# Turning the FFNs' attention probabilities with transposing transfers instead of TensorE transposes

## The chip, the cores and the metric

One core of one Trainium2 chip runs the whole kernel. The metric is device microseconds of one execution, the median of three runs. TensorE is called PE, VectorE DVE, ScalarE ACT, GpSimd POOL, SyncE SP; a "tile" is a block of 128 tokens.

## The reference, cut to what matters

```python
x = x + 0.5 * ffn(layernorm(x))
x = x + attn(layernorm(x))
x = x + 0.5 * ffn(layernorm(x))          # x: (8, 512, 256), float32

def ffn(h):                              # 16 experts, hidden size C = 256, H = 128
    w = gates(h)                         # (tokens, 16): softmax over the active experts
    def mix(proj):                       # proj: (16, C, H)
        pe = einsum('nc,ech->neh', h, proj)
        return einsum('ne,neh->nh', w, pe)
    q, k, v = mix(q_proj), mix(k_proj), mix(v_proj)
    scores = where(causal, einsum('bqh,bkh->bqk', q, k) / sqrt(H), -1e9)
    ao = einsum('bqk,bkh->bqh', softmax(scores), v)
    return einsum('enh,ehc->nc', einsum('ne,nh->enh', w, ao), o_proj)
```

Each of the two FFNs is itself an attention of one head whose projections are mixtures of 16 experts. The 16-head attention between them is not touched.

## The kernel before

Three programs follow each other: `ffn` (FFN 1), `attention`, `ffn` again (FFN 2). x stays in SBUF throughout. Products that need float32 accuracy are made of fp32r high and low halves, three matmuls each.

**An FFN as a pipeline of slots.** There are 32 tiles (8 batch items of QT = 4 tiles) and 34 slots. Slot T works on several tiles at once, and the order on each engine is written out by hand in that engine's `slot(T, t)`: a loop over e = 0 to 15, the experts, into which the steps of other tiles are set at fixed e. In slot T, PE does

- `mix(T, t, e)` (L555) for e = 1 to 15: six matmuls of 384 columns for tile T, into a ring of four PSUM banks that DVE empties with `sum_mix` (L725, L727);
- at every odd e, `project(T - 2, ..., e // 2, ...)` (L605): three matmuls of 512 columns, the output projection of tile T - 2, which DVE adds up in `sum_output` (L742, L744, L746). The first of them, at e = 1, waits for `av_lo`, the low half of that tile's attention output;
- at e = 0 `transpose_y` and at e = 2 `mix_first` for tile T + 1;
- the small causal attention of tile T - 1: `transpose_qk` at e = 4, `scores` at e = 6, `transpose_probs` (L583) at e = 9, `attend` (L593) at e = 12. "t" of a tile is its number within its batch item, 0 to 3; its scores have (t + 1) * 128 columns.

**The chain of tile T - 1 within slot T.** PE scores (e = 6); DVE `score_max` (L759, e = 7); ACT `exponentials` (L902), into `prob`, float32 in SBUF; PE `transpose_probs` turns `prob` into PSUM, t + 1 blocks of 128 by 128; ACT `split_probs` (L908, high half) and DVE `split_probs` (L765, e = 10, low half) bring them to `probT` in SBUF; PE `attend` (e = 12); DVE `sum_av` (L779, L783, e = 13) adds the two halves of the result; POOL `split_av` (L1026, L1028) makes the halves `avT`; and in slot T + 1, at e = 1, PE's first `project` reads `avT`. A tile's probabilities are unnormalised; 1 / sum goes into the output weights `w_out`.

POOL's order in a slot: `merge_qkv` and `split_v` of tile T - 1, the gate's steps for tile T + 1, `split_av(T - 1)`, `merge_x(T - 2)` (L1033). SP first loads all weights, in FFN 1 then the first pieces of the attention's weights when their space is free, and in FFN 2 stores each batch item when its four tiles are merged.

**In `attention`** the probabilities are turned already by transposing transfers: ACT (L1556) and DVE (L1479) write `probs` as two fp16 halves scaled by 2^15, SP issues `dma_start_transpose` (L1294) into `turned_long` (14 blocks of 128 columns, 1792) and `turned_short` (6 blocks, 768), and POOL casts them to fp32r (L1614).

Of the kernel before, what the change touches and what calls it, by code (L numbers as in the profile page):

```python
# [47 lines left out]
ON_POOL = (5, 7, 13)  # L48

# [220 lines left out]

def lo_of(n):

    if n in ON_POOL:
        return "pool", ON_POOL.index(n) + 1
    return "dve", n + 1 - sum(i < n for i in ON_POOL)


def ffn(nc, m, name, aw, sim_matrix, gates, q_proj, k_proj, v_proj, o_proj, x_in, out):
    with ExitStack() as ctx:
# [25 lines left out]

        stats = sb("ln_stats", [P, 2, 6])
# [37 lines left out]
        prob = sb("prob", [P, SEQ])  # L344
        p_sum = sb("prob_sum", [P, 1])
        p_rsum = sb("prob_rsum", [P, 1])
        pT = sb("probT", [P, QT, 2, P], F32R)
# [30 lines left out]
        pt_tr, pt_hi, pt_lo, av_ready = sem("pt_tr"), sem("pt_hi"), sem("pt_lo"), sem("av_rdy")  # L378
# [54 lines left out]
        def _(sp):  # L433
# [43 lines left out]
            if aw:  # L477
                for n in range(EARLY):
                    if n == 0:
                        split_done(sp, E + OG - 2)  # L480
                        split_done(sp, E + OG - 1)
                    if n == 2:
                        last_tile_past(sp, aw.first_end)
                    if n == EARLY - 2:
                        last_tile_past(sp, aw.second_end)
                    src, _, _, _, width = aw.pieces[n]
                    raw = aw.parts(n)[0]
                    sp.dma_start(raw, src).then_inc(aw.loaded[n % EARLY], 16)
            if out is not None:
                out_rows = out.rearrange("b (t p) c -> b p t c", p=P)  # L490
                with sp.Fori(0, B) as b:
                    sp.wait_ge(x_merged, b * QT + QT)
                    sp.dma_start(out_rows[bass.ds(b, 1)].rearrange("a p t c -> p (a t) c"),
                                 m.x[:, bass.ds(b * QT, QT), :]).then_inc(stored, 16)
                sp.wait_ge(stored, 16 * B)

        @block.tensor
        def _(pe):
# [136 lines left out]
        def _(dve):  # L635
# [156 lines left out]
            def slot(T, t):  # L792
                nxt, prev, nn = (t + 1) % QT, (t + 3) % QT, (t + 2) % QT
                for e in range(E):
# [33 lines left out]
                    if inside(T, 1):  # L828
                        if e == 4:
                            split_qk(T - 1, prev)  # L830
                        if e == 7:
                            score_max(T - 1, prev)
                        if e == 9:
                            prob_rsum(T - 1, prev)
                        if e == 10:
# [3 lines left out]
                        if e == 13:  # L839
# [34 lines left out]
        def _(act):  # L874
# [44 lines left out]
            def slot(T, t):  # L919
                for e in range(E):  # L920
# [12 lines left out]
                    if e == 9 and inside(T, 1):  # L933
# [22 lines left out]
        def _(pool):  # L956
# [65 lines left out]

            def split_av(T, t):
# [16 lines left out]
            def slot(T, t):  # L1040
# [21 lines left out]
                if inside(T, 1):  # L1062
                    split_av(T - 1, prev)
# [25 lines left out]
PROB_SCALE = 2.0 ** 15  # L1089
# [597 lines left out]
```

## Time and profile before

| | |
|---|---|
| median of 3 runs | 2614.89 us (2613.47 to 2616.02) |
| profiled execution | 2615.02 us |
| its span in the trace | 2613.2 us |
| TensorE busy | 2511.2 us (96%) |
| VectorE busy | 2155.9 us (83%) |
| ScalarE, GpSimd busy | 945.1 us (36%), 910.6 us (35%) |
| transposing transfers, from issue to landing | 4.0 us (1792 columns), 3.5 us (768 columns), medians |

A profile comes from one execution. Busy time is the share of the span in which an engine runs an instruction. PE's matmuls are pipelined: what one costs is the distance between the starts of groups that follow each other, not its own duration. "[x <- engine tile line]" behind a row is the idle time before it and what ended it.

### The profile page before, as it was taken

The numbers are of one execution on the slowest core, as the hardware profiler recorded it, in microseconds if no ns is written. First come the engines' busy times: TensorE is split into PE (matmuls) and PEld (weight loads), VectorE is DVE, ScalarE is ACT, GpSimd is POOL, SyncE is SP. The second block draws the span as 40 slices with busy tenths as digits, with TensorE's granted clock in tenths as the row PEclk, the third lists the DMA queues.
The fourth block names the chain that finished last, engine by engine and source line by source line (L and its number), as shares of the span: only waits on it lengthen the run. The fifth ranks groups of instructions, "written<-read, shape, count | busy, mean of one in ns | idle before, by whom it ended". The sixth has DMA issues, their size and how long they took to land. (4 is left out here: it accounts for less than half of the span.)

```text
span 2613.2 us, 45221 instructions
## 1 busy us (share of the span) xinstructions
PE 2511.2 (96%) x14116; PEld 2298.0 (88%) x14116; DVE 2155.9 (83%) x6164; ACT 945.1 (36%) x2546; POOL 910.6 (35%) x1950
## 2 busy tenths in 40 slices
PE   6999999999996899999999999997999999999998
PEld 6999999999995788888888888886899999999997
DVE  6888888888886888888888888886888888888887
ACT  3111101101102777777777777774111101101100
POOL 4332332332323444343434344334332332332321
PEclk9999999999998999999999999997999999999999
DMA  6000000000001554454545554455100000000000
GB/s 191 11 1 1 1 1 1 1 1 1 1 25 49 91 92 91 86 94 90 87 92 91 92 92 91 85 98 127 34 9 1 9 9 1 9 9 1 9 9 9
DMA packets 378735, 117.25 MB, mean 45 GB/s; under 512 B 338560, under 2 KB 377472, under 8 KB 378496
## 3 DMA queue, kind: packets, MB, share of 16 engines
q1 hardware_dynamic: 378496, 114.36, 21.9%
q8 instruction: 114, 1.87, 0.3%
q14 instruction: 125, 1.02, 0.1%
HBM read 26.24 MB, written 4.19 MB: 12 GB/s over the span
## 5 line engine op out<-in xcount | busy, mean ns | idle before, releaser
L555 PE MATMUL ffn_ring<-ffn_mix_weights,ffn_yT 128*128 128x384 f32 x5760 | 1155.7, 341 | 6.7 <-DVE ffn_mix_weights L790 4.3
L555 PEld LDWEIGHTS ffn_ring<-ffn_mix_weights,ffn_yT 128*128 128x128 f32 x5760 | 1007.4, 189 | 57.5 <-DVE ffn_mix_sums L725 15.8
L727 DVE SCALAR_TENSOR_TENSOR ffn_mix_sums<-ffn_ring,ffn_w,ffn_mix_sums 128x384 f32<-128x384 f32 x896 | 550.3, 614 | 243.0 <-PE ffn_ring L555 226.1
L605 PE MATMUL ffn_ring<-ffn_out_weights,ffn_avT 128*128 128x512 f32 x1536 | 442.3, 399 | 6.2 <-POOL ffn_avT L1028 4.5
L1547 ACT ACTIVATE attn_exponentials<-attn_exponentials,attn_score_neg_max 128x512 f32<-128x512 f32 (+3 forms) x512 | 285.8, 559 | 173.5 <-DVE attn_score_neg_max L1462 172.9
L1614 POOL CAST attn_probsT_long<-attn_turned_long 128x1024 fp32r<-128x1024 f16 (+1 forms) x256 | 232.4, 936 | 248.0 <-DVE attn_probs L1479 246.8
L605 PEld LDWEIGHTS ffn_ring<-ffn_out_weights,ffn_avT 128*128 128x128 f32 x1536 | 282.8, 189 | 36.0 <-POOL ffn_avT L1028 5.7
L1479 DVE SCALAR_TENSOR_TENSOR attn_probs<-attn_exponentials,attn_prob_factor,attn_probs 128x512 f16<-128x512 f32 (+3 forms) x512 | 254.0, 557 | 20.2 <-ACT attn_probs L1556 19.9
L1556 ACT ACTIVATE attn_probs<-attn_exponentials,attn_prob_factor 128x512 f16<-128x512 f32 (+3 forms) x512 | 250.2, 552 | 23.1 <-DVE attn_prob_factor L1472 13.8
L742 DVE SCALAR_TENSOR_TENSOR x<-ffn_ring,ffn_w_out,x 128x256 f32<-128x256 f32 x512 | 246.9, 482 | 12.0 <-PE ffn_ring L605 5.3
L1302 PE MATMUL attn_scores<-attn_kT,attn_qT 128*128 128x512 f32 (+2 forms) x1152 | 243.2, 338 | 9.1 <-DVE attn_qT L1445 7.6
L1462 DVE CUSTOM_DVE_ANT_0 attn_exponentials<-attn_scores,causal_row 128x512 f32<-128x512 f32 (+2 forms) x384 | 205.5, 551 | 32.1 <-PE attn_scores L1341 24.0
L1302 PEld LDWEIGHTS attn_scores<-attn_kT,attn_qT 128*128 128x128 f32 x1152 | 197.8, 189 | 38.2 <-DVE attn_qT L1445 8.0
L1302 PE MATMUL attn_dense<-attn_wd,attn_ctxT 128*128 128x256 f32 x1512 | 202.0, 283 | 20.6 <-DVE attn_ctxT L1486 19.4
L1302 PEld LDWEIGHTS attn_dense<-attn_wd,attn_ctxT 128*128 128x128 f32 x1512 | 185.4, 189 | 31.4 <-DVE attn_ctxT L1486 29.3
L746 DVE SCALAR_TENSOR_TENSOR ffn_out_odd<-ffn_ring,ffn_w_out,ffn_out_odd 128x256 f32<-128x256 f32 x448 | 212.7, 475 | 0.0
L1614 POOL CAST attn_probsT_short<-attn_turned_short 128x512 fp32r<-128x512 f16 (+1 forms) x256 | 122.9, 508 | 232.7 <-DVE attn_probs L1479 232.7
L1302 PE MATMUL attn_projections<-attn_zT,early_wq 128*128 128x512 f32 x768 | 201.8, 398 | 1.5 <-DVE attn_zT L1447 1.5
L884 ACT ACTIVATE ffn_yT<-ffn_transposes 128x256 fp32r<-128x256 f32 x64 | 24.5, 383 | 493.2 <-PE ffn_transposes L525 493.2
L888 ACT ACTIVATE ffn_qT<-ffn_transposes 128x128 fp32r<-128x128 f32 x64 | 17.7, 277 | 441.4 <-PE ffn_transposes L565 441.4
L1302 PE MATMUL attn_ctx<-attn_probsT_long,attn_v 128*128 128x512 f32 (+1 forms) x768 | 167.3, 366 | 0.0
L1026 POOL CAST ffn_avT<-ffn_av 128x128 fp32r<-128x128 f32 x64 | 19.5, 304 | 420.7 <-DVE ffn_av L783 420.7
(149 smaller groups left out, 3263.1 us busy)
## 6 DMA issues: line engine op xcount, KB each, us to landing
ffn_mix_stage<-in_L_ffn_q_proj_dram SPq DMA_DIRECT2D x32, 128.0 KB, 2.5
ffn_mix_stage<-in_L_ffn_k_proj_dram SPq DMA_DIRECT2D x32, 128.0 KB, 2.6
ffn_mix_stage<-in_L_ffn_v_proj_dram SPq DMA_DIRECT2D x32, 128.0 KB, 2.9
ffn_out_stage<-in_L_ffn_o_proj_dram SPq DMA_DIRECT2D x16, 256.0 KB, 3.2
out_dram<-x SPq DMA_DIRECT2D x8, 512.0 KB, 2.9
x<-in_L_attn_x_dram SPq DMA_DIRECT2D x7, 512.0 KB, 8.2
early_stage<-in_L_attn_w_q_dram SPq DMA_DIRECT2D x4, 512.0 KB, 5.7
attn_dense_stage<-in_L_attn_w_dense_dram SPq DMA_DIRECT2D x4, 512.0 KB, 4.7
```

What stands on the lines that cost most here:

```text
L555: last = pe.matmul(bank[:, 0:QKV], yT[:, t % 2, h, k * P:(k + 1) * P], mix_half(e, wh)[:, k], start=(n == 0), stop=(n == 3 * CK - 1))
L605: last = pe.matmul(bank[:], avT[:, t % 2, h], wo[:, g, wh], start=(i == 0), stop=(i == 2))
L727: dve.scalar_tensor_tensor(into, bank[:, 0:QKV], w[:, t, e:e + 1], into, ALU.mult, ALU.add).then_inc(mix_done, 1)
L742: dve.scalar_tensor_tensor(x, bank[:, 0:C], wt[:, 2 * g:2 * g + 1], x, ALU.mult, ALU.add)
L746: dve.scalar_tensor_tensor(odd[:, t % 2], bank[:, C:2 * C], wt[:, 2 * g + 1:2 * g + 2], odd[:, t % 2], ALU.mult, ALU.add).then_inc(out_don ...
L884: act.activation(yT[:, t % 2, 0], tr[:, 0:C], ACT.Copy).then_inc(yT_hi, 1)
L1302: mm = pe.matmul(out_ap, stationary(a), moving(c), start=first and n == 0, stop=last and n == 2, skip_group_check=True)
L1462: dve.tensor_tensor_reduce(expo[:, at:at + width], raw, row, -1.0, BIGGEST, ALU.add, ALU.min, s_bias[:, h % 2, i:i + 1]).then_inc(s_max, 1)
L1479: dve.scalar_tensor_tensor(prob_half(1, i), expo[:, at:at + width].rearrange("p (j k) -> p j k", k=P), p_factor[:, h % 2, i:i + 1], prob_h ...
L1547: act.activation(expo[:, at:at + width], expo[:, at:at + width], ACT.Exp, bias=s_bias[:, h % 2, i:i + 1], scale=-1.0, accum_out=p_sum[:, h ...
L1556: act.activation(prob_half(0, i), expo[:, at:at + width].rearrange("p (j k) -> p j k", k=P), ACT.Copy, scale=p_factor[:, h % 2, i:i + 1]). ...
L1614: pool.tensor_copy(cast(n, i), landed(n, i).rearrange("p (j h q) -> p j h q", h=HL, q=P)).then_inc(long_cast if pair_of(i) else short_cast, 1)
```

## The change

In each FFN, tiles 1 to 30 (`by_dma(T)`) take another path; tiles 0 and 31 keep the old one.

- PE: `transpose_probs` is left out for them, and `attend` moves from e = 12 to e = 14.
- ACT: `split_probs` is replaced by `prob16_high` at e = 8: `prob` times 2^15 as fp16, from SBUF to SBUF. It waits for the exponentials.
- DVE: `split_probs` at e = 10 is replaced by `prob16_low` at e = 9, the fp16 remainder; `sum_av` moves from e = 13 to e = 15. `w_out` takes the factor 2^-15.
- SP: `turn_probs(T)`, one `dma_start_transpose` of 2 (t + 1) blocks of 128 columns, after `pt_lo`.
- POOL: `cast_turned`, fp16 to fp32r, ahead of `split_av`.
- `turned` has the space of `prob`, `prob_halves` that of `probT`.
- SP's list is now written out: the transfers for tiles 1 to 30, with the store of a batch item behind the transfer of every fourth tile in FFN 2, and in FFN 1 the early loads 0 to 5 of the attention's weights ahead of the transfer of tile 30 and loads 6 and 7 behind it.

```diff
+def by_dma(T):
+
+    return 0 < T < TILES - 1
+
...
+        turned = nc.alloc_sbuf_tensor_at(f"{name}_prob_turned", [P, 2 * SEQ], F16, offset=nc.sbuf_base)
+        prob = sb("prob", [P, SEQ])
+        prob16 = nc.alloc_sbuf_tensor_at(f"{name}_prob_halves", [P, QT, 2, P], F16, offset=nc.sbuf_base)
+        pT = sb("probT", [P, QT, 2, P], F32R)
...
+            def turn_probs(T):
+
+                columns = 2 * (T % QT + 1) * P
+                sp.wait_ge(pt_lo, T + 1)
+                sp.dma_start_transpose(turned[:, 0:columns].rearrange("p (j q) -> p j q", q=P),
+                                       prob16[:].rearrange("p j h k -> p (j h k)")[:, 0:columns]).then_inc(t_landed, 16)
...
+            for T in range(1, TILES - 1):
+                if aw and T == TILES - 2:
+                    for n in range(EARLY - 2):
+                        load_early(n)
+                turn_probs(T)
+                if out is not None and T > QT and T % QT == 1:
+                    store((T - QT) // QT)
+            if aw:
+                load_early(EARLY - 2)
+                load_early(EARLY - 1)
...
             def attend(T, t):
 
-                pe.wait_ge(pt_hi, T + 1)
-                pe.wait_ge(pt_lo, T + 1)
+                if by_dma(T):
+                    pe.wait_ge(pt_free, T + 1)
+                    pe.wait_ge(av_done, T)
+                else:
+                    pe.wait_ge(pt_hi, T + 1)
+                    pe.wait_ge(pt_lo, T + 1)
...
-                    if e == 9 and inside(T, 1):
+                    if e == 9 and inside(T, 1) and not by_dma(T - 1):
                         transpose_probs(T - 1, (t + 3) % QT)
-                    if e == 12 and inside(T, 1):
+                    if inside(T, 1) and e == (14 if by_dma(T - 1) else 12):
                         attend(T - 1, (t + 3) % QT)
...
+            def prob16_low(T, t):
+                n = (t + 1) * P
+                dve.wait_ge(pt_hi, T + 1)
+                dve.scalar_tensor_tensor(prob16[:, 0:t + 1, 1], prob[:, 0:n].rearrange("p (j k) -> p j k", k=P), PROB_SCALE,
+                                         prob16[:, 0:t + 1, 0], ALU.mult, ALU.subtract).then_inc(pt_lo, 1)
...
+                        if e == 9 and by_dma(T - 1):
+                            prob16_low(T - 1, prev)
                         if e == 9:
                             prob_rsum(T - 1, prev)
-                        if e == 10:
+                        if e == 10 and not by_dma(T - 1):
                             split_probs(T - 1, prev)
                         if e == 11:
                             output_weights(T - 1, prev)
-                        if e == 13:
+                        if e == (15 if by_dma(T - 1) else 13):
                             sum_av(T - 1, prev)
...
+            def prob16_high(T, t):
+                n = (t + 1) * P
+                act.wait_ge(exp_done, T + 1)
+
+                act.wait_ge(av_ready, T)
+                act.activation(prob16[:, 0:t + 1, 0], prob[:, 0:n].rearrange("p (j k) -> p j k", k=P), ACT.Copy,
+                               scale=PROB_SCALE).then_inc(pt_hi, 1)
...
+            def cast_turned(T, t):
+                pool.wait_ge(t_landed, 16 * T)
+
+                pool.wait_ge(av_ready, T)
+                pool.tensor_copy(pT[:, 0:t + 1].rearrange("p j h q -> p (j h q)"),
+                                 turned[:, 0:2 * (t + 1) * P]).then_inc(pt_free, 1)
...
                 if inside(T, 1):
+                    if by_dma(T - 1):
+                        cast_turned(T - 1, prev)
                     split_av(T - 1, prev)
```

**PE, from the projection at e = 11 of a slot whose previous tile has t = 3, to the mixture at e = 2 of the next slot.** `ffn_ring<-ffn_mix_weights` is `mix`, `ffn_ring<-ffn_out_weights` is `project`, `ffn_probs_av<-ffn_probT` is `attend`, `ffn_transposes<-ident,ffn_y` opens the next slot. Before:

```order
L605 MATMUL ffn_ring<-ffn_out_weights,ffn_avT 128x512 x3
L555 MATMUL ffn_ring<-ffn_mix_weights,ffn_yT 128x384 x6
L593 MATMUL ffn_probs_av<-ffn_probT,ffn_v 128x256 x8
L555 MATMUL ffn_ring<-ffn_mix_weights,ffn_yT 128x384 x6
L605 MATMUL ffn_ring<-ffn_out_weights,ffn_avT 128x512 x3
L555 MATMUL ffn_ring<-ffn_mix_weights,ffn_yT 128x384 x12
L605 MATMUL ffn_ring<-ffn_out_weights,ffn_avT 128x512 x3
L525 MATMUL ffn_transposes<-ident,ffn_y 128x128 x2
L555 MATMUL ffn_ring<-ffn_mix_weights,ffn_yT 128x384 x6
L605 MATMUL ffn_ring<-ffn_out_weights,ffn_avT 128x512 x3
L555 MATMUL ffn_ring<-ffn_mix_weights,ffn_yT 128x384 x6
```

and with the change:

```order
L637 MATMUL ffn_ring<-ffn_out_weights,ffn_avT 128x512 x3
L583 MATMUL ffn_ring<-ffn_mix_weights,ffn_yT 128x384 x12
L637 MATMUL ffn_ring<-ffn_out_weights,ffn_avT 128x512 x3
L583 MATMUL ffn_ring<-ffn_mix_weights,ffn_yT 128x384 x6
L625 MATMUL ffn_probs_av<-ffn_probT,ffn_v 128x256 x8
L583 MATMUL ffn_ring<-ffn_mix_weights,ffn_yT 128x384 x6
L637 MATMUL ffn_ring<-ffn_out_weights,ffn_avT 128x512 x3
L553 MATMUL ffn_transposes<-ident,ffn_y 128x128 x2
L583 MATMUL ffn_ring<-ffn_mix_weights,ffn_yT 128x384 x6
L637 MATMUL ffn_ring<-ffn_out_weights,ffn_avT 128x512 x3
L583 MATMUL ffn_ring<-ffn_mix_weights,ffn_yT 128x384 x6
```

Between `attend` and the next slot's first `project` (the last but one row), which reads what comes of it, there stood four mixtures, two projections and the transposes of y; now there stand two mixtures, one projection and those transposes.

**DVE, from e = 13 of a slot to e = 0 of the next.** Before:

```order
L699 TENSOR_REDUCE ffn_gate_sum<-ffn_gate_kept 128x1
L779 COPY ffn_av_half<-ffn_probs_av 128x128
L783 TENSOR_TENSOR ffn_av<-ffn_probs_av,ffn_av_half 128x128
L727 SCALAR_TENSOR_TENSOR ffn_mix_sums<-ffn_ring,ffn_w,ffn_mix_sums 128x384
L703 RECIPROCAL ffn_gate_rsum<-ffn_gate_sum 128x1
L727 SCALAR_TENSOR_TENSOR ffn_mix_sums<-ffn_ring,ffn_w,ffn_mix_sums 128x384
L742 SCALAR_TENSOR_TENSOR x<-ffn_ring,ffn_w_out,x 128x256
L746 SCALAR_TENSOR_TENSOR ffn_out_odd<-ffn_ring,ffn_w_out,ffn_out_odd 128x256
L707 TENSOR_SCALAR ffn_w<-ffn_gate_kept,ffn_gate_rsum 128x16
L725 TENSOR_SCALAR ffn_mix_sums<-ffn_first_expert,ffn_w 128x384
```

and with the change:

```order
L731 TENSOR_REDUCE ffn_gate_sum<-ffn_gate_kept 128x1
L759 SCALAR_TENSOR_TENSOR ffn_mix_sums<-ffn_ring,ffn_w,ffn_mix_sums 128x384
L735 RECIPROCAL ffn_gate_rsum<-ffn_gate_sum 128x1
L759 SCALAR_TENSOR_TENSOR ffn_mix_sums<-ffn_ring,ffn_w,ffn_mix_sums 128x384
L774 SCALAR_TENSOR_TENSOR x<-ffn_ring,ffn_w_out,x 128x256
L778 SCALAR_TENSOR_TENSOR ffn_out_odd<-ffn_ring,ffn_w_out,ffn_out_odd 128x256
L739 TENSOR_SCALAR ffn_w<-ffn_gate_kept,ffn_gate_rsum 128x16
L817 COPY ffn_av_half<-ffn_probs_av 128x128
L821 TENSOR_TENSOR ffn_av<-ffn_probs_av,ffn_av_half 128x128
L757 TENSOR_SCALAR ffn_mix_sums<-ffn_first_expert,ffn_w 128x384
```

`sum_av` (the copy and the sum of `ffn_probs_av`) has moved behind the last mixture and the last projection of the slot.

## Rows read from the trace of the kernel before

**Rows 1.** Windows: a slot of FFN 1, and the end of FFN 1.
```profile
core 0: us, PE busy (x) PEld busy (x) DVE busy (x) ACT busy (x) POOL busy (x), PEclk, DMA share, GB/s
506.23:531.29 25.06, 25.06 (x140) 23.56 (x139) 20.42 (x55) 3.06 (x9) 7.60 (x21) 1.00 0.00 1
800.00:818.00 18.00, 10.69 (x47) 7.14 (x45) 15.28 (x30) 1.59 (x5) 13.43 (x12) 1.00 0.00 0
```

**Rows 2.** Timeline of PE, 521 to 533 us: start, us, what.
```profile
521.52 0.60 PE L583 MATMUL ffn_probs_av<-ident,ffn_prob 128*128 128x128 f32 x4
...
524.07 0.86 PE L605 MATMUL ffn_ring<-ffn_out_weights,ffn_avT 128*128 128x512 f32 x3
...
525.82 1.11 PE L593 MATMUL ffn_probs_av<-ffn_probT,ffn_v 128*128 128x256 f32 x8
526.77 1.21 PE L555 MATMUL ffn_ring<-ffn_mix_weights,ffn_yT 128*128 128x384 f32 x6
...
528.51 2.25 PE L555 MATMUL ffn_ring<-ffn_mix_weights,ffn_yT 128*128 128x384 f32 x12
530.60 0.86 PE L605 MATMUL ffn_ring<-ffn_out_weights,ffn_avT 128*128 128x512 f32 x3
531.29 0.38 PE L525 MATMUL ffn_transposes<-ident,ffn_y 128*128 128x128 f32 x2
...
532.56 0.86 PE L605 MATMUL ffn_ring<-ffn_out_weights,ffn_avT 128*128 128x512 f32 x3
```

**Rows 3.** Timeline of DVE, 522 to 533 us.
```profile
522.52 0.17 DVE L689 MAX8 ffn_gate_key_top<-ffn_gate_key 128x8 f32<-128x16 f32 x1
...
528.08 0.62 DVE L727 SCALAR_TENSOR_TENSOR ffn_mix_sums<-ffn_ring,ffn_w,ffn_mix_sums 128x384 f32<-128x384 f32 x1 [1.29 <-PE ffn_ring L555]
...
529.58 0.28 DVE L779 COPY ffn_av_half<-ffn_probs_av 128x128 f32<-128x128 f32 x1
529.97 0.29 DVE L783 TENSOR_TENSOR ffn_av<-ffn_probs_av,ffn_av_half 128x128 f32<-128x128 f32 x1
...
531.49 0.48 DVE L742 SCALAR_TENSOR_TENSOR x<-ffn_ring,ffn_w_out,x 128x256 f32<-128x256 f32 x1
...
532.29 0.23 DVE L707 TENSOR_SCALAR ffn_w<-ffn_gate_kept,ffn_gate_rsum 128x16 f32<-128x16 f32 x1
```

**Rows 4.** Timeline of POOL, 530 to 532 us.
```profile
530.39 0.29 POOL L1026 CAST ffn_avT<-ffn_av 128x128 fp32r<-128x128 f32 x1 [6.75 <-DVE ffn_av L783]
530.76 0.46 POOL L1028 TENSOR_TENSOR ffn_avT<-ffn_av,ffn_avT 128x128 fp32r<-128x128 f32 x1
```

**Rows 5.** Timelines of POOL, PE and DVE at FFN 2's end, one row each.
```profile
2598.95 0.45 POOL L1028 TENSOR_TENSOR ffn_avT<-ffn_av,ffn_avT 128x128 fp32r<-128x128 f32 x1
...
2599.46 7.39 PE L605 MATMUL ffn_ring<-ffn_out_weights,ffn_avT 128*128 128x512 f32 x24 [1.82 <-POOL ffn_avT L1028]
...
2600.52 0.48 DVE L742 SCALAR_TENSOR_TENSOR x<-ffn_ring,ffn_w_out,x 128x256 f32<-128x256 f32 x1 [1.29 <-PE ffn_ring L605]
```

**Rows 6.** Timeline of ACT, 520 us.
```profile
520.43 0.72 ACT L902 ACTIVATE ffn_prob<-ffn_prob,ffn_score_bias 128x512 f32<-128x512 f32 x1 [2.44 <-DVE ffn_score_bias L759]
```

**Rows 7.** Groups by shape, 860 to 1790 us: count, busy us, mean ns, idle before.
```profile
L1614 POOL CAST attn_probsT_long<-attn_turned_long 128x1024 fp32r<-128x1024 f16 x128 | 133.4, 1043 | 248.0 <-DVE attn_probs L1479 246.8 <-issue 1.2
...
L1479 DVE SCALAR_TENSOR_TENSOR attn_probs<-attn_exponentials,attn_prob_factor,attn_probs 128x512 f16<-128x512 f32 x126 | 94.4, 749 | 14.8 <-ACT attn_probs L1556 14.5
...
L1556 ACT ACTIVATE attn_probs<-attn_exponentials,attn_prob_factor 128x512 f16<-128x512 f32 x126 | 90.3, 717 | 12.7 <-DVE attn_prob_factor L1472 6.7 <-DMA attn_turned_long<-attn_probs 5.1 <-DVE attn_prob_rsum L1470 0.7
```

**Rows 8.** Landings of the transposing transfers: tile turned_long (1792 columns), then turned_short (768).
```profile
DMA to landing us min/median/max: 4.0/4.0/5.8
...
DMA to landing us min/median/max: 2.8/3.5/5.4
```

**Rows 9.** Timeline of PE, 812 us, the end of FFN 1.
```profile
812.50 3.07 PE L605 MATMUL ffn_ring<-ffn_out_weights,ffn_avT 128*128 128x512 f32 x12 [2.67 <-POOL ffn_avT L1028]
```

**Rows 10.** Line L605, the whole run: duration ns min/median/max.
```profile
L605 PE MATMUL ffn_ring<-ffn_out_weights,ffn_avT x1536: 388/397/795, 69.7 to 2606.5; 128*128 128x512 f32 x192
```

More of the change, by code:

```diff
@@ L48 @@
 ON_POOL = (5, 7, 13)
+PROB_SCALE = 2.0 ** 15
 class Resident:
@@ L343, in ffn @@
         s_bias = sb("score_bias", [P, 1])
-        prob = sb("prob", [P, SEQ])
         p_sum = sb("prob_sum", [P, 1])
         p_rsum = sb("prob_rsum", [P, 1])
-        pT = sb("probT", [P, QT, 2, P], F32R)
         av_half = sb("av_half", [P, P])
@@ L377, in ffn @@
         p_rsum_done = sem("p_rsum")
-        pt_tr, pt_hi, pt_lo, av_ready = sem("pt_tr"), sem("pt_hi"), sem("pt_lo"), sem("av_rdy")
+        pt_free, pt_hi, pt_lo, av_ready = sem("prob_free"), sem("pt_hi"), sem("pt_lo"), sem("av_rdy")
+        t_landed = sem("prob_landed")
         av_half_done, av_done, av_hi, av_lo = sem("av_half"), sem("av"), sem("av_hi"), sem("av_lo")
@@ L476, in _ @@
                 load_out(g)
[L477 to L488, printed above, removed]
+            def turn_probs(T):
[3 more added lines that the diff above has]
+                                       prob16[:].rearrange("p j h k -> p (j h k)")[:, 0:columns]).then_inc(t_landed, 16)
@@ L489, in _, with load_early @@
+            def load_early(n):
+                if n == 0:
+                    split_done(sp, E + OG - 2)
+                    split_done(sp, E + OG - 1)
+                if n == 2:
+                    last_tile_past(sp, aw.first_end)
+                if n == EARLY - 2:
+                    last_tile_past(sp, aw.second_end)
+                src, _, _, _, width = aw.pieces[n]
+                sp.dma_start(aw.parts(n)[0], src).then_inc(aw.loaded[n % EARLY], 16)
             if out is not None:
@@ L490, in _, with store @@
                 out_rows = out.rearrange("b (t p) c -> b p t c", p=P)
[L491 to L494, printed above, removed]
+            def store(b):
+                sp.wait_ge(x_merged, b * QT + QT)
+                sp.dma_start(out_rows[b], m.x[:, b * QT:b * QT + QT, :]).then_inc(stored, 16)
@@ L495, in _ @@
+            for T in range(1, TILES - 1):
[8 more added lines that the diff above has]
+                load_early(EARLY - 1)
+            if out is not None:
+                store(B - 1)
                 sp.wait_ge(stored, 16 * B)
@@ L583, in transpose_probs @@
                     last = pe.transpose(pt[:, j * P:(j + 1) * P], prob[:, j * P:(j + 1) * P], m.ident[:])
-                last.then_inc(pt_tr, 1)
+                last.then_inc(pt_free, 1)
             def attend(T, t):
-                pe.wait_ge(pt_hi, T + 1)
-                pe.wait_ge(pt_lo, T + 1)
+                if by_dma(T):
[4 more added lines that the diff above has]
+                    pe.wait_ge(pt_lo, T + 1)
                 pe.wait_ge(v_lo, T + 1)
@@ L756, in score_max @@
                 dve.wait_ge(scores_ready, T + 1)
-                reach(dve, pt_tr, T)
+                reach(dve, pt_free, T)
                 settle(dve)
@@ L774, in output_weights @@
                 dve.wait_ge(p_rsum_done, T + 1)
-                dve.tensor_scalar(w_out[:, t % 2], w[:, t], p_rsum[:, 0:1], 0.5, ALU.mult, ALU.mult).then_inc(w_out_done, 1)
+                dve.tensor_scalar(w_out[:, t % 2], w[:, t], p_rsum[:, 0:1], 0.5 / PROB_SCALE if by_dma(T) else 0.5, ALU.mult, ALU.mult).then_inc(w_out_done, 1)
             def sum_av(T, t):
@@ L906, in split_probs @@
                 n = (t + 1) * P
-                act.wait_ge(pt_tr, T + 1)
+                act.wait_ge(pt_free, T + 1)
                 act.activation(pT[:, 0:t + 1, 0], pt[:, 0:n].rearrange("p (j q) -> p j q", q=P), ACT.Copy).then_inc(pt_hi, 1)
+            def prob16_high(T, t):
[4 more added lines that the diff above has]
+                               scale=PROB_SCALE).then_inc(pt_hi, 1)
             def split_weights(n):
@@ L932, in slot @@
                         exponentials(T - 1, (t + 3) % QT)
-                    if e == 9 and inside(T, 1):
+                    if e == 8 and inside(T, 1) and by_dma(T - 1):
+                        prob16_high(T - 1, (t + 3) % QT)
+                    if e == 9 and inside(T, 1) and not by_dma(T - 1):
                         split_probs(T - 1, (t + 3) % QT)
@@ L1088 @@
 LAST_LAG = 4
-PROB_SCALE = 2.0 ** 15
 PROB_AT = (0, P, 3 * P, 6 * P)
```

## Prediction

> **What bounds the kernel now.** I read the windows first, then the timelines of one slot engine by engine, and the groups by shape last. The window over one slot of FFN 1, the one in which the previous tile has t = 3, has PE busy for all of its 25.06 us, DVE for 20.42, ACT for 3.06 and POOL for 7.60 [rows 1]. So in an FFN's slot PE never stops, and every matmul taken out of it is worth its full distance; DVE is second, and it catches up with PE again and again, since it sits idle 1.29 us for the mixture at e = 13 [rows 3]. ACT and POOL wait most of the time. What counts for this change is therefore (1) how much PE work goes, and (2) whether any wait that PE passes freely today turns into one that it sits in. The candidates are the two places where PE reads what the small attention makes: `attend` and the next slot's first `project`.
>
> **What goes from PE.** From the start of the four transposes at 521.52 to the projection at 524.07 are 2.55 us, and in them lie four transposes and twelve mixture matmuls. Twelve mixture matmuls alone take from 528.51 to 530.60, 2.09 us [rows 2]. So a transpose costs 0.46 / 4 = 0.115 us of PE. Tiles 1 to 30 of an FFN have 7 tiles with t = 0, 8 with t = 1, 8 with t = 2 and 7 with t = 3, in all 7 + 16 + 24 + 28 = 75 blocks; both FFNs 150. The gain is 150 * 0.115 = 17 us, and since PE is never idle there it would come off the time in full.
>
> **The move of `attend` and `sum_av`: the term that decides.** Let S be the end of the slot's last projection, 531.29 in [rows 2]. Today the attention output of tile T - 1 is complete in its halves at 530.76 + 0.46 = 531.22 [rows 4], and PE comes to the `project` that reads it at 532.56, S + 1.27 [rows 2]: 1.34 us to spare. The change puts `attend` two experts later, and on DVE the sum of its halves behind everything that belongs to e = 15, which itself waits for the last mixture and the last projection. The new chain, from rows of today's slot:
>
> - DVE adds the last projection to x at 531.49, S + 0.20, directly behind its sum of the last mixture (that mixture's end at 530.60, the 0.27 us from a mixture's end to DVE, 528.51 - 0.70 = 527.81 to 528.08, and 0.62 us give the same 531.49) [rows 2, 3];
> - the two sums of the projection take until L707 starts at 532.29, 0.80 us more; L707 takes up to 0.23 us [rows 3];
> - the copy, then 0.39 us later the sum of the halves (529.58 to 529.97) [rows 3];
> - from the start of that sum to POOL's cast 0.42 us (529.97 to 530.39), to POOL's subtraction 0.37, and 0.46 for it [rows 3, 4];
> - from its end to PE 0.06 us (2598.95 + 0.45 to 2599.46) [rows 5].
>
> That is 0.20 + 0.80 + 0.23 + 0.39 + 0.42 + 0.37 + 0.46 + 0.06 = 2.93 us behind S, where PE arrives at S + 1.27. PE would wait 1.66 us. The copy may start before L707 has ended, which takes off up to 0.1 us. On the other side, a projection that starts from a standstill is slower: from 2599.46 to 0.20 us before DVE's 2600.52 are 0.86 us [rows 5], against 0.69 to 0.70 for one in the stream (530.60 to 531.29) [rows 2], 0.16 more. I take 1.75 us a slot. Nothing in it depends on t, because both the chain and PE's arrival are counted from S. It happens for every tile that goes by transfer, 30 in each FFN: 60 * 1.75 = 105 us. Nothing hides it: the chain is released by PE's own last projection, so PE cannot build up a lead over it, and PE's order is fixed, so it stands in front of `project` with the next mixtures behind it. After that wait DVE has caught up, POOL's `merge_x` and `merge_qkv` come about 1.6 us later, but PE needs them only at e = 4.
>
> **The turned probabilities: late or not?** For t = 3, the tightest case, in today's times. DVE's key maximum starts at 522.52, and the low half right behind it, at 522.6 [rows 3]; the high half on ACT follows the exponentials, from 520.43 for 0.72 us, and takes 0.72 for 512 columns, so that with hand-overs it is done by 522.1 [rows 6, 7]. The low half takes 0.75, to 523.35 [rows 7]. Then SP's wait and issue start, 0.2 (an estimate from DVE's and POOL's reactions of 0.1 to 0.3 above), the transfer, 0.1, the cast of 1024 columns, 1.04 [rows 7], and 0.1 to PE. The transfer is not in this trace in this size: 768 columns land after 2.8 us at best, 1792 after 4.0 [rows 8]. By columns 1024 would be 3.1, and I take that, as 1024 is nearer to 768. Ready: 523.35 + 0.2 + 3.1 + 0.1 + 1.04 + 0.1 = 527.9. PE comes to `attend` at 528.51 + 1.04 (the mixture at e = 14) - 0.95 (`attend` today, 525.82 to 526.77) - 0.46 (transposes) = 528.14 [rows 2]. In time by 0.25 us; with 4.0 for the transfer, late by 0.65 in the 14 slots with t = 3 and by some 0.2 in the 16 with t = 2, 12 us together. I take 0 and keep 12 for the range. The Trainium skill (DMA: Bandwidth & Descriptors, the tables of fixed cost and of measured facts) gives about 2.0 us fixed and 261 GB/s for a transposing transfer; an estimate by it is 3.0 us for this size, and by it the sum stays as it is.
>
> **At nothing.** DVE: the low half costs 0.75 us for 512 columns in place of today's sum from PSUM, on an engine with 4.6 us idle in the slot [rows 1, 7]. ACT and POOL: 0.72 and 1.04 us at most per slot, covered by 22 and 17 us of idle time [rows 1, 7]; POOL's cast ends before the sum that `split_av` waits for, so it is not in that one's way. SP: in FFN 2 a store stands behind the transfer of every fourth tile and waits for merges that are a slot old; the early loads in FFN 1 go out at the start of slot 31, about nine experts ahead of the transfer of tile 30. Each has only the next slot's transfer behind it. If that cover failed for tile 30, it would cost a few us once.
>
> **The sum.** The profiled execution is 2615.0 us (0.1 over the median, so I take it as it is): 2615 - 17 + 105 + 0 = 2703 us, 3.4% slower. A measurement of this kernel can tell about 0.2%, some 5 us.
>
> **Rivals.**
> 1. *The transfer is the wait.* If landing takes 5.8 us, the longest in the trace [rows 8], `attend` is late by about 2.4 us at t = 3 and not much less for the others (their casts are shorter, and so is their `attend`); 2 us in 60 slots on top are 2823 us. Against it: 5.8 is one end of 128 transfers whose median is 4.0, and the queue here is empty, where there two transfers follow each other. Chance 0.05.
> 2. *The output chain is hidden, and the kernel is faster.* Its place is the first `project` of a slot, its price zero, and it decides where the chain is shorter than PE's 1.27 us behind S. Then only the transposes count: 2598 us. For it speaks that today this wait is passed 1.34 us early. Against it, the sums of the last projection and the two steps on POOL alone make 0.20 + 0.80 + 0.83 = 1.83 us. Chance 0.03.
> 3. *The clock falls.* A stall in every slot could bring PE to 1.2 GHz for a while; one projection matmul at the low level takes up to 795 ns, double the usual 397 [rows 10]. If one projection and one mixture after each stall ran so, it would cost another 0.70 + 1.04 = 1.74 us a slot, 2808 us. Against it: from 800 to 818 us PE is busy only 10.69 of 18 us, with a pause of 2.67 us [rows 9], and the granted clock is 1.00, the level of 2.4 GHz [rows 1]. The Trainium skill (TensorE: Matmul & The Clock Gate, "A second HAM failure mode: psum-queue depth-cycling") says that frequent short pauses between groups of matmuls can make the clock swing between its levels; by that rule this rival holds, and the window just named speaks against it. Chance 0.04.
> 4. *The change does little*, since most tiles keep the old path or the wait is partly filled: 2615 within 5 us. 60 of 64 tiles change, so 0.01.
>
> The forecast has the rest, 0.87. **Range:** with 1.4 us a slot (each hand-over a little shorter) 2682; with 2.0 us and 12 us for the transfers 2730. Half of the latencies are read from one slot, and some part of rival 1 is likely when it comes, so I take 2672 to 2750. Faster has rival 2 and a rest, 0.04; same 0.02; slower 0.94.
>
> **What would show it.** In the changed kernel's profile PE should have an idle time of about 1.6 us before the first `project` of nearly every slot, ended by POOL's low half of `avT`, 90 to 105 us in all; no idle time, or some tenths at t = 3 only, before `attend`; slots of about 25.3 us for t = 0 to 26.3 for t = 3; a landing near 3 us; the granted clock 1.00 within the FFNs; and the attention phase as before. I am wrong if that idle time is missing, if PE waits for `probT` (rival 1), or if matmuls are longer with the clock below 1.00 (rival 3).

## The result, and the profile after

The changed kernel takes **2696.3 us** (median of 6 runs, 2694.3 to 2697.7), the kernel before 2612.9 beside it (6 runs, 2610.7 to 2616.0). The ratio is 1.0317, with an interval of 1.0305 to 1.0329: 3.2% slower, 83 us where the forecast said 88.

The page of the changed kernel, its head and part 1 (busy us, share, count), and its row for the projection from part 5 (busy us, mean ns, idle before it):

```profile
span 2695.0 us, 45058 instructions
...
PE 2508.6 (93%) x13966; PEld 2288.5 (85%) x13966; DVE 2168.5 (80%) x6164; ACT 947.6 (35%) x2546; POOL 955.8 (35%) x2010
...
L637 PE MATMUL ffn_ring<-ffn_out_weights,ffn_avT 128*128 128x512 f32 x1536 | 450.2, 404 | 91.7 <-POOL ffn_avT L1085 91.2
```

PE has 150 instructions fewer, and almost the same busy time as before, but 3% of its time has become idle. Where, the waits of PE tell (engine, line, releaser: us in total, times, longest), after:

```profile
PE ffn_ring L637 <- POOL ffn_avT L1085: 91.2, 62, 2.7
```

and in the kernel before, for the same wait:

```profile
PE ffn_ring L605 <- POOL ffn_avT L1028: 4.5, 2, 2.7
```

The two that were there before are the ends of the FFNs [rows 5, 9]; the 60 new ones are the 60 tiles that go by transfer: 55 of them wait 1.39 to 1.40 us, one 1.65, and the last two of each FFN, where PE no longer has the next tile's transposes, and at last no mixture either, to fill the time, 1.61 and 2.52 us. The other candidate of the forecast, `attend`, hardly waits: 0.9 us in 2 times.

Windows of two slots of FFN 1 in the changed kernel, the first with t = 2 for the previous tile, the second with t = 3 (it answers to the slot of [rows 1]):

```profile
core 0: us, PE busy (x) PEld busy (x) DVE busy (x) ACT busy (x) POOL busy (x), PEclk, DMA share, GB/s
...
503.20:528.96 25.76, 24.36 (x134) 22.86 (x133) 20.78 (x55) 2.88 (x9) 8.48 (x22) 1.00 0.04 9
528.96:555.14 26.18, 24.79 (x136) 23.17 (x135) 20.67 (x55) 3.10 (x9) 8.83 (x22) 1.00 0.06 11
```

PE executes four matmuls fewer than in [rows 1] (136 for 140), is busy for 24.79 us instead of 25.06, and the slot is 1.12 us longer, at the same granted clock of 1.00. The four transposes took 0.46 us, so the slot pays 1.12 + 0.46 = 1.58 us for something new.

Timeline of PE at the end of that slot (start, us, what, and in brackets the idle time before it with its releaser); S, the end of the slot's last projection, is 555.14:

```profile
552.45 1.11 PE L625 MATMUL ffn_probs_av<-ffn_probT,ffn_v 128*128 128x256 f32 x8
553.40 1.21 PE L583 MATMUL ffn_ring<-ffn_mix_weights,ffn_yT 128*128 128x384 f32 x6
554.45 0.86 PE L637 MATMUL ffn_ring<-ffn_out_weights,ffn_avT 128*128 128x512 f32 x3
555.14 0.38 PE L553 MATMUL ffn_transposes<-ident,ffn_y 128*128 128x128 f32 x2
555.28 1.29 PE L583 MATMUL ffn_ring<-ffn_mix_weights,ffn_yT 128*128 128x384 f32 x6
557.97 0.96 PE L637 MATMUL ffn_ring<-ffn_out_weights,ffn_avT 128*128 128x512 f32 x3 [1.40 <-POOL ffn_avT L1085]
558.77 0.51 PE L583 MATMUL ffn_ring<-ffn_mix_weights,ffn_yT 128*128 128x384 f32 x2
```

DVE in the same stretch:

```profile
554.72 0.62 DVE L759 SCALAR_TENSOR_TENSOR ffn_mix_sums<-ffn_ring,ffn_w,ffn_mix_sums 128x384 f32<-128x384 f32 x1 [1.31 <-PE ffn_ring L583]
555.34 0.48 DVE L774 SCALAR_TENSOR_TENSOR x<-ffn_ring,ffn_w_out,x 128x256 f32<-128x256 f32 x1
555.75 0.47 DVE L778 SCALAR_TENSOR_TENSOR ffn_out_odd<-ffn_ring,ffn_w_out,ffn_out_odd 128x256 f32<-128x256 f32 x1
556.14 0.23 DVE L739 TENSOR_SCALAR ffn_w<-ffn_gate_kept,ffn_gate_rsum 128x16 f32<-128x16 f32 x1
556.27 0.28 DVE L817 COPY ffn_av_half<-ffn_probs_av 128x128 f32<-128x128 f32 x1
556.66 0.29 DVE L821 TENSOR_TENSOR ffn_av<-ffn_probs_av,ffn_av_half 128x128 f32<-128x128 f32 x1
```

and POOL (its first row is the cast of the turned probabilities, whose end at 551.81 is 0.64 us ahead of `attend`):

```profile
550.77 1.04 POOL L1077 CAST ffn_probT<-ffn_prob_turned 128x1024 fp32r<-128x1024 f16 x1 [2.56 <-DMA ffn_prob_turned<-ffn_prob_halves]
557.08 0.29 POOL L1083 CAST ffn_avT<-ffn_av 128x128 fp32r<-128x128 f32 x1 [5.27 <-DVE ffn_av L821]
557.46 0.46 POOL L1085 TENSOR_TENSOR ffn_avT<-ffn_av,ffn_avT 128x128 fp32r<-128x128 f32 x1
```

The output of `attend` lies in PSUM from about 553.4 on, and DVE is idle for 1.31 us before 554.72. But the copy stands in DVE's order behind the last mixture and the last projection, so it runs at 556.27. From S the chain is 0.20 + 0.80 + 0.13 + 0.39 + 0.42 + 0.38 + 0.46 + 0.05 = 2.83 us (PE restarts at 557.97), and PE would be there at S + 1.27. The two landmarks of before, L783 at 529.97 and L1028 at 530.76 with S at 531.29 [rows 2 to 4], have moved from before S to 1.5 and 2.3 us behind it.

The new transfer, its tile `ffn_prob_turned`:

```profile
DMA to landing us min/median/max: 2.3/2.7/4.5
```

By size they land after 2.4 us (t = 0, 256 columns), 2.5 (t = 1), 2.8 (t = 2) and 3.1 (t = 3, 1024 columns), medians, with a few late ones, and the cast for t = 3 is mostly done 0.64 to 0.71 us before PE comes to `attend`.

The granted clock is 1.00 in all slots in which every part of the pipeline is at work, but not up to the FFNs' ends. Behind the last new pause of FFN 1, and in the same way behind that of FFN 2 at 2667.52, it falls for a stretch (PE's timeline, and a window around it):

```profile
837.66 2.04 PE L637 MATMUL ffn_ring<-ffn_out_weights,ffn_avT 128*128 128x512 f32 x6 [2.52 <-POOL ffn_avT L1085]
```
```profile
836.00:846.00 10.00, 6.62 (x22) 4.69 (x23) 6.84 (x21) 1.26 (x4) 8.85 (x13) 0.83 0.00 1
```

### The profile page after: what moved, and what is told of

It reads as the page before. It is cut to its first block and busy times, and to the rows that moved or that the text cites. A ratio compares the mean times of both kernels' runs of the same rounds, so it can differ in the third digit from the quotient of the medians.

```text
span 2695.0 us, 45058 instructions
## 1 busy us (share of the span) xinstructions
PE 2508.6 (93%) x13966; PEld 2288.5 (85%) x13966; DVE 2168.5 (80%) x6164; ACT 947.6 (35%) x2546; POOL 955.8 (35%) x2010
## 3 DMA queue, kind: packets, MB, share of 16 engines
q14 instruction: 128, 1.05, 0.1%
## 5 line engine op out<-in xcount | busy, mean ns | idle before, releaser
L637 PE MATMUL ffn_ring<-ffn_out_weights,ffn_avT 128*128 128x512 f32 x1536 | 450.2, 404 | 91.7 <-POOL ffn_avT L1085 91.2
L1360 PEld LDWEIGHTS attn_projections<-attn_zT,early_wq 128*128 128x128 f32 x768 | 143.9, 191 | 25.2 <-DVE attn_zT L1505 1.9
```

The source lines that it names most:

```text
L637: last = pe.matmul(bank[:], avT[:, t % 2, h], wo[:, g, wh], start=(i == 0), stop=(i == 2))
L1360: mm = pe.matmul(out_ap, stationary(a), moving(c), start=first and n == 0, stop=last and n == 2, skip_group_check=True)
```

## The experiments

Their ratios are to the kernel before, timed on the same chip in turn with them (its medians there: 2613.4 us, 9 runs, for the first four; 2614.2 us, 14 runs, for the last three). My theory: the whole loss is where `sum_av` stands on DVE. The rivals: `attend`'s own move or the transfer costs something too, or the transfers bring something less than the transposes' price.

**1. The sum one expert earlier.** On the changed kernel, `sum_av` at the end of e = 14 instead of e = 15; nothing else.

```
-if e == (15 if by_dma(T - 1) else 13):
+if e == (14 if by_dma(T - 1) else 13):
```

> The changed kernel with one edit: DVE's sum_av stands at the end of e = 14, ahead of the sums of the last mixture and the last projection, and no longer behind them. Theory (the output chain is late because sum_av waits behind e = 15): it is then released by attend itself. From attend's end 0.2 us to the copy, 0.39, 0.42, 0.37 and 0.46 to the low half and 0.06 to PE are 1.90 us, and PE comes to the first project 3.0 us after attend (a mixture, a projection, the transposes of y, a mixture): no wait. All 91 us of idle time before the first project go, and what is left is the gain of the transposes, 17 us: about 2597 us, faster than both kernels by 0.6% and 3.7%. Rival (the transfer or the move of attend is what costs): most of the 83 us stay, 2680 us or more. Rival 3 (DVE, now waiting for attend at e = 14, becomes late for the ring): PE waits for mixture sums, some tenths of a us in each slot, 2600 to 2625 us.

Measured: **2599.8 us** (2595.3 to 2602.6), ratio 0.9945, interval 0.9932 to 0.9959. It is 96.5 us faster than the changed kernel and 13.6 us faster than the kernel before. The slot with t = 3, windows, and then DVE, POOL and PE around S = 527.45, timelines:

```profile
502.85:527.45 24.60, 24.60 (x136) 23.15 (x135) 20.69 (x55) 3.10 (x9) 8.88 (x23) 1.00 0.06 13
```
```profile
525.91 0.29 DVE L817 COPY ffn_av_half<-ffn_probs_av 128x128 f32<-128x128 f32 x1 [0.19 <-PE ffn_probs_av L625]
526.30 0.29 DVE L821 TENSOR_TENSOR ffn_av<-ffn_probs_av,ffn_av_half 128x128 f32<-128x128 f32 x1
527.02 0.62 DVE L759 SCALAR_TENSOR_TENSOR ffn_mix_sums<-ffn_ring,ffn_w,ffn_mix_sums 128x384 f32<-128x384 f32 x1 [0.43 <-PE ffn_ring L583]
```
```profile
527.10 0.47 POOL L1085 TENSOR_TENSOR ffn_avT<-ffn_av,ffn_avT 128x128 fp32r<-128x128 f32 x1
```
```profile
527.45 0.38 PE L553 MATMUL ffn_transposes<-ident,ffn_y 128*128 128x128 f32 x2
527.59 1.29 PE L583 MATMUL ffn_ring<-ffn_mix_weights,ffn_yT 128*128 128x384 f32 x6
528.72 0.63 PE L637 MATMUL ffn_ring<-ffn_out_weights,ffn_avT 128*128 128x512 f32 x2
```

The copy now uses the idle time in front of the last mixture's sum, the low half is ready at 527.57, and PE passes the projection at 528.72 with 1.15 us to spare. PE is busy for the whole slot again, and the slot is 24.60 us: the 25.06 of [rows 1] less 0.46, to the hundredth. `attend` stands at e = 14 here as in the changed kernel, so its own move costs nothing. So the loss is one line's place on DVE.

**2. The moves alone.** On the kernel before, its transposes on TensorE left in: `attend` at e = 14 and `sum_av` at e = 15 for tiles 1 to 30.

```
-if e == 12 and inside(T, 1):
+if inside(T, 1) and e == (14 if 0 < T - 1 < TILES - 1 else 12):
-if e == 13:
+if e == (15 if 0 < T - 1 < TILES - 1 else 13):
```

> The kernel before, with attend at e = 14 and sum_av at e = 15 for tiles 1 to 30, and nothing else: the probabilities are still turned on TensorE, there is no transfer, no cast, no fp16. Theory (the places alone make the loss): the same wait before the first project, 1.4 to 1.6 us in 60 slots, and no gain from transposes: 2613 + 95 = about 2708 us, slower than the changed kernel by the 17 us of the transposes less a few. Rival (transfer, cast or the shared work on GpSimd make the loss): near 2613 us.

Measured: 2712.2 us (2711.5 to 2716.9), ratio 1.0377, interval 1.0361 to 1.0392. The waits of PE:

```profile
PE ffn_ring L605 <- POOL ffn_avT L1028: 91.3, 62, 2.7
```

That is the changed kernel's wait to 0.1 us, without any transfer in the FFNs. The moves cost 98.8 us, or 1.65 in each of 60 slots, and the rest of the change (transfers, halves, casts, no transposes) is 2696.3 - 2712.2 = -16 us, close to the 17 of 150 transposes.

**3. The transfers in the old places.** On the changed kernel: `attend` at e = 12 and `sum_av` at e = 13 for all tiles.

```
-if inside(T, 1) and e == (14 if by_dma(T - 1) else 12):
+if inside(T, 1) and e == 12:
-if e == (15 if by_dma(T - 1) else 13):
+if e == 13:
```

> The changed kernel with attend back at e = 12 and sum_av at e = 13. Theory: the output chain is in time again, but the turned probabilities are not. In the changed kernel the cast ends 0.7 us (t = 3), 1.3 (t = 2), 2.0 (t = 1) and 2.5 us (t = 0) before PE comes to attend; two mixtures and a projection earlier are 2.8 us, so PE waits before attend 2.1, 1.5, 0.8 and 0.3 us: 14*2.1 + 16*1.5 + 16*0.8 + 14*0.3 = 70 us, and 2597 + 70 = 2667 us. Rival (a transfer that starts earlier is no faster, and places do not matter): as the changed kernel, 2696 us. Rival 2 (the transfers cost nothing anywhere): 2597 us.

Measured: 2698.3 us (2694.9 to 2701.1), ratio 1.0322, interval 1.0307 to 1.0338. **Here my expectation missed** by 31 us, although the wait that it was built on came out right (70 expected):

```profile
PE ffn_probs_av L625 <- POOL ffn_probT L1077: 72.4, 60, 2.8
```

Windows of two slots, with t = 2 and t = 3:

```profile
608.70:634.51 25.81, 24.43 (x135) 22.77 (x133) 20.78 (x55) 2.88 (x9) 8.54 (x22) 1.00 0.04 9
634.51:662.96 28.45, 26.42 (x136) 24.51 (x135) 20.49 (x55) 3.10 (x9) 8.87 (x22) 0.94 0.05 10
```

and PE's timeline in the second:

```profile
655.84 1.22 PE L625 MATMUL ffn_probs_av<-ffn_probT,ffn_v 128*128 128x256 f32 x8 [2.03 <-POOL ffn_probT L1077]
656.89 2.02 PE L583 MATMUL ffn_ring<-ffn_mix_weights,ffn_yT 128*128 128x384 f32 x6
658.70 1.49 PE L637 MATMUL ffn_ring<-ffn_out_weights,ffn_avT 128*128 128x512 f32 x3
659.98 2.44 PE L583 MATMUL ffn_ring<-ffn_mix_weights,ffn_yT 128*128 128x384 f32 x12
662.27 0.86 PE L637 MATMUL ffn_ring<-ffn_out_weights,ffn_avT 128*128 128x512 f32 x3
```

Two things were not in the sum. First, a pause costs more than the idle time listed. The window with t = 2 is 25.81 us against 24.17 of the same kind of slot in run 1, 1.64 more, with 1.39 us of idle listed: 0.25 more per pause. (The list counts idle time from a modelled end of the last matmul, which is later than where the next would have started.) Over 60 pauses that is about 15 us. Second, the clock: the slot with t = 3 is 28.45 us against 24.60 in run 1, 3.85 more, with 2.03 listed. Behind the pause six mixture matmuls take 1.81 us up to the next row's start instead of 1.04 to 1.05, three projection matmuls 1.28 instead of 0.70, and the window's granted clock is 0.94: for a stretch PE ran at 1.2 GHz. Subtracting 0.25, that is 1.6 us. The clock fell like this in 7 of the 14 slots with t = 3, about 11 us together (7 times 1.6). 15 + 11 are 26 of the 31 us; the idle time itself was 2 us over the 70, and run 1, which the sum started from at 2597, came out 3 us above that. So with a transfer `attend` can't stay at e = 12: there it waits in every one of the 60 slots.

**4. Transposes doubled.** On the kernel before, each block of the probabilities turned twice into the same place, 160 more matmuls of that kind.

```
-for j in range(t + 1):
+for j in [*range(t + 1)] * 2:
```

> The kernel before, with each of its 160 transposes of probabilities done twice into the same place: the price of a transpose on TensorE by itself. Theory: PE never waits in a slot, so 160 more at 0.115 us each are 18 us: 2631 us. If a transpose hides behind other work (its weights are loaded while a matmul runs): less, down to 2613 us.

Measured: 2630.5 us (2627.8 to 2632.3), ratio 1.0063, interval 1.005 to 1.0077: 17.1 us more, 0.107 us for a transpose, against the 0.115 read from [rows 2].

**5. The sum between the last mixture and the last projection.** On the changed kernel, `sum_av` stays at e = 15 but ahead of the projection's two sums on DVE.

```
+if e == 15 and inside(T, 1) and by_dma(T - 1):
+    sum_av(T - 1, prev)
 if e % 2 and inside(T, 2):
...
-if e == (15 if by_dma(T - 1) else 13):
+if e == 13 and not by_dma(T - 1):
```

> The changed kernel with sum_av between the sum of the last mixture (e = 15) and the sums of the last projection. If the wait before the first project is the sum of its links, this takes out 0.80 us for the projection's sums and 0.13 for the gate's weights: the low half is ready 1.90 us behind the end of the last projection, PE comes after 1.27, and the idle time of 1.40 us in each of 60 slots becomes about 0.5. 2696 - 60*0.93 = 2640 us. If the wait has another cause (GpSimd busy, a shared port), it shrinks less or not at all: 2680 us or more.

Measured: 2632.4 us (2632.0 to 2634.9), ratio 1.0064, interval 1.0049 to 1.008. The waits of PE, and DVE and PE in one slot, S = 538.47:

```profile
PE ffn_ring L637 <- POOL ffn_avT L1087: 29.4, 62, 2.1
```
```profile
538.04 0.62 DVE L759 SCALAR_TENSOR_TENSOR ffn_mix_sums<-ffn_ring,ffn_w,ffn_mix_sums 128x384 f32<-128x384 f32 x1 [1.31 <-PE ffn_ring L583]
538.58 0.28 DVE L817 COPY ffn_av_half<-ffn_probs_av 128x128 f32<-128x128 f32 x1
538.96 0.29 DVE L821 TENSOR_TENSOR ffn_av<-ffn_probs_av,ffn_av_half 128x128 f32<-128x128 f32 x1
```
```profile
540.27 0.95 PE L637 MATMUL ffn_ring<-ffn_out_weights,ffn_avT 128*128 128x512 f32 x3 [0.37 <-POOL ffn_avT L1087]
```

The projection comes at S + 1.80, and 1.03 us earlier than in the changed kernel (S + 2.83). I had expected 1.90. The copy starts at 538.58, when the instruction in front of it is listed until 538.66: a DVE instruction starts a little before the recorded end of the one ahead of it, which I had not taken off. 64 us of the loss come back, 1.07 a slot. (By the ratios, each to the kernel before beside it, it is 66 us.)

**6. The sum ahead of the gate's weights.** On the changed kernel, `sum_av` behind the last projection's sums but ahead of `gate_weights`' L739.

```
+if inside(T, 1) and by_dma(T - 1):
+    sum_av(T - 1, prev)
 gate_weights(...)
...
-if e == (15 if by_dma(T - 1) else 13):
+if (e == 15 and by_dma(T - 1) and not inside(T, -1)) or (e == 13 and not by_dma(T - 1)):
```

> The changed kernel with sum_av ahead of the gate's weights at e = 15, behind everything else: one short link less, 0.13 us by the trace of the changed kernel (529.96 to 530.09). 60*0.13 = 8 us: 2688 us, if every link counts in full; 2696 us if not.

Measured: 2689.2 us (2685.5 to 2689.4), ratio 1.0276, interval 1.0262 to 1.029. The wait is 82.5 us, and the projection stands at S + 2.69: PE's row for S = 553.14,

```profile
555.83 0.95 PE L637 MATMUL ffn_ring<-ffn_out_weights,ffn_avT 128*128 128x512 f32 x3 [1.26 <-POOL ffn_avT L1087]
```

so L739 costs the chain 0.14 us and not its listed 0.23. The time is 7 us below the changed kernel's, 11 by the ratios, where 8 were expected. Runs 5 and 6 move the chain's start by two different amounts, and the time follows both.

**7. Both one expert earlier.** On the changed kernel, `attend` at e = 13 and `sum_av` at e = 14 for the tiles that go by transfer.

```
-if inside(T, 1) and e == (14 if by_dma(T - 1) else 12):
+if inside(T, 1) and e == (13 if by_dma(T - 1) else 12):
-if e == (15 if by_dma(T - 1) else 13):
+if e == (14 if by_dma(T - 1) else 13):
```

> The changed kernel with attend at e = 13 and sum_av at e = 14, each one expert earlier. The output chain has then more than 2 us to spare. attend comes one mixture, 1.04 us, earlier than in the changed kernel, where the cast ended 0.7 us before it at t = 3, 1.3 at t = 2 and 2 or more for the others: PE should wait 0.35 us in the 14 slots with t = 3, and a start from a standstill costs it another 0.1 to 0.25. With sum_av at e = 14 alone 2600 us was measured, so 2600 + 14*0.55 = 2608 us. If pauses of 2 us are what brings the clock down, as in the kernel with the old places, it stays at 1.00 here; if any pause does it in some slots, 2620 us.

Measured: 2609.9 us (2606.5 to 2612.7), ratio 0.9979, interval 0.997 to 0.9989. PE now waits for the turned probabilities 16 times, in all 14 slots with t = 3 and in two with t = 2; the waits, and one row of a slot:

```profile
PE ffn_probs_av L625 <- POOL ffn_probT L1077: 5.4, 16, 1.1
```
```profile
526.69 1.22 PE L625 MATMUL ffn_probs_av<-ffn_probT,ffn_v 128*128 128x256 f32 x8 [0.27 <-POOL ffn_probT L1077]
```

It is some 9 us slower than run 1 (3.4 thousandths of ratio). Of the versions run, `attend` at e = 14 with the sum at the end of the same e is the one to keep.

## Why the prediction was right, step by step

**What bounds the kernel: right.** In the window of run 1, 0.46 us off PE's work are 0.46 us off the slot, and in run 4 work added to PE lengthens the kernel by its price.

**Transposes, 150 * 0.115 = 17 us: right.** Three readings agree: 0.46 in the slot of run 1, 0.107 apiece where they were doubled, and 16 us between run 2 and the changed kernel. As an end-to-end gain, run 1 has 13.6 us. Of the missing 3 to 4, 1.7 lie in three of its slots that are 0.56, 0.30 and 0.86 us longer than their like, and in each of them the transfer lands late, after 4.5, 3.9 and 4.4 us; the rest is not assigned.

**The output chain, 60 * 1.75 = 105 us: the place and the mechanism right, the size a tenth too large.** Run 2 shows that the moves alone make it, run 1 that the sum's place alone takes it away. By links, 2.83 us against the 2.93 of the forecast: all are within 0.01 us but the one for L707, now L739, taken at 0.23 and measured at 0.13 (556.14 to 556.27). The text had named this overlap, "up to 0.1 us", but its 1.75 lies between 1.72, with the overlap taken off in full, and 1.82 without it. Runs 5 and 6 measured it two more times. The slow restart is 0.80 us from 557.97 to 558.77 instead of 0.70, so 0.10 more and not 0.16; the 0.86 that it was read from [rows 5] lies at FFN 2's end. Together 1.56 + 0.10 = 1.66 us, of which the window shows 1.58 net. 60 * 1.58 - 17 are 78 us, against 82 between the two profiled spans and 83 between the medians. Of the remaining 4 us, 1.8 are three slots with a late transfer (landing after 4.4, 3.9 and 4.5 us; 0.45, 0.33 and 0.99 us longer than their like), and 0.4 is the attention, 972.9 us after 972.5; about 2 us are not assigned.

Nothing in the term was to depend on t, and that is so: the slots came out at 25.08, 25.35, 25.76 and 26.18 us where the previous tile has t = 0 to 3 (25.3 to 26.3 was said), and with their transposes added back each is 1.58 to 1.60 us longer than before. The exceptions are the waits at each FFN's end, up to 2.52 us. My listed idle time was to be "about 1.6 us" and 90 to 105 in all; it is 1.40 each and 86.7 for the 60 new ones (91.2 with the two old ones), since the list starts at the modelled end of the last matmul.

**The transfer, 0 us: right, and nearer the good end.** 1024 columns land after 3.1 us, as the scale by columns between the sizes of [rows 8] had said. The slack is 0.64 us rather than 0.25. The low half starts where it was expected, 5.54 us before `attend` (546.91 to 552.45), but ends after 0.67 us and not 0.75; SP's wait cost 0.04 us and not 0.2 (it issues at 547.62); from there the cast starts after 3.15 us and not 3.2; and the last 0.1 us of the sum, from the cast to PE, lies within the 0.64. The Trainium skill (DMA: Bandwidth & Descriptors) led to an estimate of 3.0 us; the rows agree. Of the 12 us kept for late transfers, 1.8 were needed. Run 3 shows what they would have cost: more than their listed idle.

**At nothing: right.** In the slot DVE, ACT and POOL stay at 20.67, 3.10 and 8.83 us busy of 26.18, and run 1, with the same work on them, has no idle time on PE in its slot.

**Rivals.** The first, the transfer as the wait, fell: 0.9 us of wait in the changed kernel, though 12 of its 60 transfers land about 0.3 to 1.7 us later than the median of their size. The second, a hidden chain, is false for this kernel but true for run 1, and that version gives 2599.8 us where the rival was priced at 2598. Its condition, a chain shorter than PE's 1.27 us behind S, was the right one: with the sum at the end of e = 14 the chain ends at S + 0.12. The third, the falling clock, did not come at the pauses of 1.4 us, but the sign "1.00 within the FFNs" failed at their ends, behind the two pauses of 2.52 us. And its chance was held low by a window that stops too early: [rows 1] ends at 818.00, and the next 11 us of the kernel before are

```profile
818.00:829.00 11.00, 5.97 (x18) 3.79 (x17) 6.71 (x15) 1.19 (x2) 2.28 (x5) 0.68 0.13 40
```

The clock falls from 818.44 on, 6 us behind the pause of 2.67 us, with another of 1.48 us between. So that the slots kept 1.00 did not follow from the window named, and was in part luck. Run 3 shows that the rival wasn't far: at t = 3, with pauses of about 2.0 us instead of 1.4, the clock fell in half of them. The rule of the Trainium skill that the forecast set beside it (TensorE: Matmul & The Clock Gate, "A second HAM failure mode: psum-queue depth-cycling") holds in half of run 3's slots with t = 3, and not with the changed kernel's pauses of 1.4 us. The fourth, little effect, fell.

## What to carry to other kernels

When a consumer is moved later to give its operand time, move what comes after it only as far as it must go, and place it by the waits around it: here one step on DVE, put behind two instructions that the bound engine itself releases, turned a gain of 14 us into a loss of 83. Count a hand-over chain from the event that releases it and compare it with where the bound engine stands at that time; short links on two engines that both have idle time made 1.6 us a slot. And don't price a pause on the bound engine by the idle time listed alone: here it cost 0.2 to 0.3 us more each, and from 2 us on sometimes the clock as well. Last, a window that is to show that something does not happen must reach some us past the event.

## What the runs showed of the hardware that I had not expected

- *The clock after short pauses.* In run 3, in the 14 slots with t = 3, the granted clock fell behind seven pauses of 1.96 to 2.42 us on an otherwise busy PE; behind the other seven, of 1.97 to 2.82 us, it did not. In the changed kernel it never fell behind the 55 pauses with 1.4 us listed, and did behind both of 2.52 us. What decides between the seven and the other seven was not found.
- *DVE and POOL hold each other up.* A small operation that took at most 0.18 us in all 64 tiles of the kernel before takes up to 0.72 us in 10 tiles of the changed kernel, beside the new cast, and both end within 0.03 us of each other; the timelines of DVE and POOL in the changed kernel:

```profile
524.51 0.72 DVE L727 TENSOR_TENSOR ffn_gate_kept<-ffn_gate_exp,ffn_gate_chosen 128x16 f32<-128x16 f32 x1
```
```profile
524.38 0.82 POOL L1077 CAST ffn_probT<-ffn_prob_turned 128x768 fp32r<-128x768 f16 x1 [2.26 <-DMA ffn_prob_turned<-ffn_prob_halves]
```

  The other way round, a small comparison on POOL that starts during DVE's low half ends 0.3 us after it, at 0.69 us (median of the 64: 0.50 us, and 0.44 in the kernel before):

```profile
546.91 0.67 DVE L803 SCALAR_TENSOR_TENSOR ffn_prob_halves<-ffn_prob,ffn_prob_halves 128x512 f16<-128x512 f32 x1
```
```profile
547.21 0.69 POOL L1053 TENSOR_SCALAR ffn_gate_fallback<-ffn_gate_key,ffn_gate_key_top,ffn_gate_idle 128x16 f32<-128x16 f32 x1 [2.85 <-DVE ffn_gate_key_top L721]
```

  The first fits what the Trainium skill says (SBUF — State Buffer, "SBUF: two separate sides"): a DVE operation with two SBUF inputs and a GpSimd operation that reads SBUF share a pair of ports, and the one that starts second waits for the whole of the other. Here DVE's idle time in every slot hid it; it was not tested by an experiment of its own.
- *Back to back on DVE.* An instruction starts about 0.1 us before the recorded end of the one ahead of it (0.08 in run 5, 538.58 against 538.66; 0.10 in the changed kernel, 556.27 against 556.37), so the sum of durations along one engine is too long by that for each.
